# A three-hop graph kernel: a group's relation rows and mask move from SyncE's queue to ScalarE's, and ScalarE's step distances grow by three

## The reference

```python
for _ in range(N_HOPS):                       # 3
    h = agg[head]
    t = agg[tail]
    left = h @ q_w
    right = jnp.tanh(rel * t @ k_w)           # rel = edge_emb[edge_type]
    att = jnp.sum(left * right, axis=1)
    e = jnp.exp(att - segment_max(att, head)[head])
    w = e / segment_sum(e, head)[head]
    summed = segment_sum(w[:, None] * rel * t, head)
    agg = summed / jnp.maximum(cnt, 1.0)[:, None]
    agg = agg / jnp.maximum(jnp.linalg.norm(agg, axis=1, keepdims=True), 1e-12)
    out = out + agg + entity_emb
```

## Time and profile before

| | |
|---|---|
| median of three runs | 11539.55 us |
| span of the profiled execution | 11570.2 us |
| PE busy | 8077.2 us (70%) |
| DVE busy | 6642.3 us (57%) |
| POOL busy | 6401.1 us (55%) |
| ACT busy | 6199.6 us (54%) |
| hop 0, first to last mask operation (L1839, 416 of them) | 3015 to 5782 us |
| hops 1 and 2, first to last copy of relation rows (L1944, 832 of them) | 5874 to 11483 us |

### The profile page before, as it was taken

How to read it: one execution, slowest core, us unless ns; L and a number is a source line. 1 busy time by engine, 2 the same in 40 slices (tenths; PEclk the granted TensorE clock), 3 DMA queues, 4 the chain that set the end, 5 groups by cost and what they waited for, 6 DMA issues and landing times. The chain is left out here.

```text
span 11570.2 us, 241070 instructions
## 1 busy us (share of the span) xinstructions
PE 8077.2 (70%) x47197; PEld 6146.6 (53%) x47197; DVE 6642.3 (57%) x27980; ACT 6199.6 (54%) x15908; POOL 6401.1 (55%) x6757
## 2 busy tenths in 40 slices
PE   2666666666688888888866666666666666666665
PEld 2444444444466666666645555555554555555554
DVE  4666666665555565655655555555554555555556
ACT  1666666666355555555545555555554555555554
POOL 4566666664455555555545555555545555555553
PEclk8776677767788999999978888888888888888887
DMA  2111111111455555555544444444434444444443
GB/s 68 43 43 43 43 43 42 43 43 41 123 176 176 177 176 176 177 175 176 176 124 139 138 138 138 137 139 136 138 118 134 136 138 137 138 136 136 137 136 112
DMA packets 1180950, 1401.16 MB, mean 121 GB/s; under 512 B 216215, under 2 KB 883640, under 8 KB 1180472
## 3 DMA queue, kind: packets, MB, share of 16 engines
q1 hardware_dynamic: 963734, 951.33, 25.8%
q0 software_dynamic: 216064, 444.28, 14.2%
q10 hardware_dynamic: 876, 2.56, 0.1%
HBM read 888.87 MB, written 183.76 MB: 93 GB/s over the span
## 5 line engine op out<-in xcount | busy, mean ns | idle before, releaser
L622 POOL DMA_INDIRECT tails<-node_rows,idx x4992 | 4715.4, 945 | 3803.9 <-remote 1610.6
L1798 DVE SCALAR_TENSOR_TENSOR acc<-acc,fade,banks 128x129 f32 x4992 | 1741.7, 349 | 2100.6 <-remote 1310.5
L1902 PE MATMUL banks<-rt,weight_t 128*128 128x129 f32 x9984 | 1674.8, 315 | 749.1 <-DVE acc L1798 724.3
L622 POOL DMA_INDIRECT l_rows<-in_x_dram,l_idx x1664 | 1591.9, 957 | 1075.1 <-issue 453.6
L1951 ACT ACTIVATE weight<-att,low 128x128 f32<-128x128 f32 x4992 | 1593.0, 391 | 1058.6 <-DVE low L1822 577.1
L1902 PEld LDWEIGHTS banks<-rt,weight_t 128*128 128x128 f32 x9984 | 1483.3, 223 | 849.8 <-issue 795.8
L1887 PE MATMUL banks<-rtt,k_sb 128*128 128x512 f32 x2496 | 1505.3, 685 | 533.8 <-issue 441.7
L1872 PE MATMUL banks<-right,window 128*128 128x128 f32 x9984 | 1567.3, 307 | 281.8 <-DVE tile_low L1814 163.4
L1814 DVE CUSTOM_DVE_ANT_0 att<-banks,agg 128x128 f32<-128x128 f32 x4992 | 1152.8, 287 | 982.6 <-remote 768.9
L1872 PEld LDWEIGHTS banks<-right,window 128*128 128x128 f32 x9984 | 1430.9, 221 | 358.3 <-DVE tile_low L1814 227.5
L1929 ACT ACTIVATE right<-banks 128x512 f32<-128x512 f32 x1248 | 730.5, 585 | 809.3 <-remote 639.2
(11 more groups left out here) (317 smaller groups left out, 9961.5 us busy)
## 6 DMA issues: line engine op xcount, KB each, us to landing
window<-qt SPq DMA_DIRECT2D x4992, 64.0 KB
agg<-pairs_kept SPq DMA_DIRECT2D x832, 384.0 KB
pairs_kept<-agg SPq DMA_DIRECT2D x416, 384.0 KB
rows_in<-tile_rows SPq DMA_DIRECT2D x208, 512.0 KB
tails<-node_rows,idx POOLq DMA_INDIRECT x4992
l_rows<-in_x_dram,l_idx POOLq DMA_INDIRECT x1664
node_rows<-agg SPq DMA_DIRECT2D x6, 1024.0 KB, 6.0
node_rows<-agg SPq DMA_DIRECT2D x3, 1088.0 KB, 8.2
```

The lines of the kernel that those rows point to most:

```text
L622: e.indirect_dma_start(out=rows[:, g, t, :], out_offset=None, in_=of, in_offset=bass.IndirectOffsetOnAxis(ap=idx[:, b, first + t:first + t ...
L1798: e.scalar_tensor_tensor(to, to, fade[:, g2, t:t + 1], bank[b_acc + t // 2][:, t % 2 * WIDE:t % 2 * WIDE + WIDE], ALU.mult, ALU.add).then_ ...
L1902: mm = s.e.matmul(bank[b_acc + t // 2][:, t % 2 * WIDE:t % 2 * WIDE + WIDE], weight_t[:, s.slot(lag, 2), t, :], rt[:, s.slot(lag, RING), t ...
```

## The change

SP's pair load (hops 1 and 2) and pair store (hop 0) become `load_pair` and `store_pair` in `scalar_hop`, issued from ACT. In hops 1 and 2 the load stands last in ACT's step at lag 0, and all other lags of ACT grow by three: so the load of group `i` is issued three of ACT's steps ahead of the copy of group `i`. In hop 0 ACT's lags stay, and the store is at lag 3 in place of 5. The store's semaphores form a ring of eight in place of four, ACT's pipeline is written for one more step of depth, and `scalar_q` gets a closing wait, since ACT may now load into `agg`'s memory only after PE has read it.

```diff
                 def sync_hop(s):
-                    if s.live(0):
+                    if first and s.live(0) and s.i % 2 == 0:
                         g4 = s.slot(0, UNROLL)
-                        if first:
...
-                        else:
-                            g8 = s.slot(0, RING)
-                            of = kept(s, 0)
-                            s.wait_ge((s_min, done(RING, GROUP)), apart=True)
-                            s.e.dma_start(pair[:, g8, :], of).then_inc(s_pair[g8].h, 16)
...
-                    if first and s.live(5):
-                        g4, g8 = s.slot(5, UNROLL), s.slot(5, RING)
-                        to = kept(s, 5)
-                        s.wait_ge((s_copied, done(5)))
-                        s.e.dma_start(to, pair[:, g8, :]).then_inc(s_keep[g4].h, 16)
...
-                        s.wait_ge((s_row[g4 // 2], ring_count(lag, UNROLL, 16)), (s_keep[g4], ring_count(lag + RING, UNROLL, 16)))
+                        s.wait_ge((s_row[g4 // 2], ring_count(lag, UNROLL, 16)), (s_keep[g8], ring_count(lag + RING, RING, 16)))
...
+                def store_pair(s, lag):
+                    if s.live(lag):
+                        g8 = s.slot(lag, RING)
+                        to = kept(s, lag)
+                        s.wait_ge((s_copied, done(lag)))
+                        s.e.dma_start(to, pair[:, g8, :]).then_inc(s_keep[g8].h, 16)
+
+                def load_pair(s, lag):
+                    if s.live(lag):
+                        g8 = s.slot(lag, RING)
+                        of = kept(s, lag)
+                        s.wait_ge((s_min, done(lag + RING, GROUP)), apart=True)
+                        s.e.dma_start(pair[:, g8, :], of).then_inc(s_pair[g8].h, 16)
+
                 def scalar_hop(s):
-                    scalar_idx(s, others, idx, s_rt, 2)
+                    scalar_idx(s, others, idx, s_rt, 2 if first else 5)
                     if first:
+                        store_pair(s, 3)
                         tanh(s, 3)
                         fading(s, 5)
                         copy_products(s, 2)
...
                     else:
-                        copy_relations(s, 0)
-                        tanh(s, 4)
-                        fading(s, 7)
-                        copy_weights(s, 7)
-                        exponents(s, 5)
-                        copy_products(s, 2)
+                        copy_relations(s, 3)
+                        tanh(s, 7)
+                        fading(s, 10)
+                        copy_weights(s, 10)
+                        exponents(s, 8)
+                        copy_products(s, 5)
+                        load_pair(s, 0)
...
+                    e.wait_ge(s_qturned.h, s_qturned.at(node_groups))
...
-                        pipeline(e, f"ha{hop}", scalar_hop, z.slot_groups, deep + 2, (TURN, GROUP * TURN) if first else (TURN, 2 * TURN, GROUP * TURN), TURN)
+                        pipeline(e, f"ha{hop}", scalar_hop, z.slot_groups, deep + 3, (TURN, GROUP * TURN) if first else (TURN, 2 * TURN, GROUP * TURN), TURN)
```

More of the change, by code:

```diff
@@ L1706, in _ @@
                     mm.then_inc(s_across.h, 1)
-        s_row = [sem(f"s_row{i}") for i in range(UNROLL)]
+        s_given.base, s_kept.base = 64, 16
+        s_row = [s_given, s_kept]
         s_win = [sem(f"s_win{i}") for i in range(UNROLL)]
@@ L1718, in gnn_two_layers @@
         pairs_kept = dram("pairs_kept", (z.slot_groups * P * KEEP,))
-        s_keep = [sem(f"s_keep{i}") for i in range(UNROLL)]
+        s_keep = [sem(f"s_keep{i}") for i in range(RING)]
         s_copied = sem("s_copied")
@@ L1734, in gnn_two_layers @@
                 rt = tensor(ctx, f"rt{hop}", [P, RING, GROUP, WIDE])
-                s_pair = s_row + s_keep
+                s_pair = s_keep
                 window = tensor(ctx, f"window{hop}", [P, UNROLL, GROUP, P])
@@ L1763, in sync_hop @@
                 def sync_hop(s):
-                    if s.live(0):
+                    if first and s.live(0) and s.i % 2 == 0:
                         g4 = s.slot(0, UNROLL)
-                        if first:
[L1767 to L1771, removed]
-                        else:
-                            g8 = s.slot(0, RING)
-                            of = kept(s, 0)
-                            s.wait_ge((s_min, done(RING, GROUP)), apart=True)
-                            s.e.dma_start(pair[:, g8, :], of).then_inc(s_pair[g8].h, 16)
+                        at = s.at(lambda i: GROUP * 2 * P * i)
+                        s.wait_ge((s_oht, done(UNROLL - 1)))
+                        s.e.dma_start(rows_in[:, g4:g4 + 2, :, :, :].rearrange("q u t w p -> q (u t w p)"),
+                                      trows[bass.ds(at, 2 * GROUP * 2 * P)].partition_broadcast(P)).then_inc(s_row[g4 // 2].h, 16)
                     if s.live(2):
@@ L2040, in vector_nodes @@
                             for s in s_keep:
-                                e.wait_ge(s.h, 16 * z.slot_groups // UNROLL)
+                                e.wait_ge(s.h, 16 * z.slot_groups // RING)
                         for a, b in zip(thirds, thirds[1:]):
@@ L2064, in _ @@
                         e.wait_ge(s_qt.h, s_qt.at(node_groups))
-                        pipeline(e, f"hs{hop}", sync_hop, z.slot_groups, deep, (TURN,) if first else (TURN, GROUP * TURN), TURN)
+                        pipeline(e, f"hs{hop}", sync_hop, z.slot_groups, deep, (TURN,), TURN)
                         if first:
                             for s in s_keep:
-                                e.wait_ge(s.h, 16 * z.slot_groups // UNROLL)
+                                e.wait_ge(s.h, 16 * z.slot_groups // RING)
                         if hop < HOPS - 1:
@@ L2103, in gnn_two_layers @@
                     s.base += z.slot_tiles
-                for s in s_row[0:2] + s_keep if first else s_pair:
-                    s.base += 16 * z.slot_groups // (UNROLL if first else RING)
+                for s in s_row if first else ():
+                    s.base += 16 * z.slot_groups // UNROLL
+                for s in s_keep:
+                    s.base += 16 * z.slot_groups // RING
                 for s in s_win:
```

## The result

The changed kernel took 11485.92 us (median of four runs, 11462.44 to 11492.87) beside 11538.52 us of the kernel before (four runs): a ratio of 0.9948, 95% interval 0.9934 to 0.9963. That is 53 us, where 645 were forecast.

A forecast was written before the change was run, and what follows sets the result against it. The prediction took SP's issuing of windows and pair loads as the bound. Gains of 541 us (hops 1 and 2) and 104 us (hop 0) made 645 us, giving 10900 us; 8-in-10 range 10350 to 11600 us.

The forecast's parts named there:

- The pace is common to the hops: Hops 0 and 1 take 6.68 and 6.69 us a group, so something that both share sets the pace.
- SP is a full engine and sets the pace: SP issues windows and loads without semaphore pauses at 6.62 us a group in hop 1, the pace of the hop.
- the term of 541 us: Gain in hops 1 and 2: 0.65 us for each of 832 groups, from 6.69 to 6.04 us.
- ACT's wait for the load is a ceiling of 1033.5 us: Hops 1 and 2: removing ACT's wait before its relation copy can shorten the whole by at most 1033.5 us.
- DVE's floor: DVE needs 3.52 us busy plus 2.09 us of waits expected to stay: 5.61 us a group.
- ACT gains nothing in work: The pair's instructions on ACT cost 0 beyond its idle time of 3.18 us a group; bounds 0 and 1.98 us.
- the sign of being wrong: ACT idle before the relation copy or the tanh for more than before would mean its issues are slow.
- the rival in which ACT pays: The pair's instructions run as slowly on ACT as on SP: 11600 us and above, likeliest 11650; chance 0.15.
- Hop 0: Gain of 0.25 us for each of 416 groups, 104 us, with PE near its own limit there.
- It is hidden: DVE's stalls grow by what ACT's wait loses; time within 0.2% of 11540 us; chance 0.06.
- only the issues are saved: SP saves only the pair's DMA issue time, 283 us and 47 us: 11210 us, stretch 11100 to 11500; chance 0.14.

The follow-up runs named there:

- half of the gathers: Two of POOL's four tail gathers a group left out in the hops: changed kernel 8847.50 us (ratio 0.7666), kernel before 8865.79 us (0.7680).
- quick chip: Chip on which the kernel before takes about 8875 us; both kernels rerun unaltered on one: changed 8867.97 us, before 8872.53 us, ratio 0.9997.
- slow chips: Chips on which the kernel before takes about 11540 us, among them that of the result.
- the leash of 6: Changed kernel, POOL's gathers in the hops waiting for `s_rtt` of six groups back in place of four: 13221.58 us, ratio 1.1468, on a slow chip.
- three gathers: Three of POOL's four tail gathers a group in the hops: kernel before 9977.25 us (0.8648, slow chip), changed kernel 8285.58 us (0.9332, quick chip).

## Why the prediction was wrong

- *The pace is common to the hops.* Right, and the best of its observations. What they share is POOL's four gathers. The prediction named POOL only to reject a rival, and priced it at 0.945 us a gather. From start to start it is 1.25 us, 5.0 us a group: with the pause, the whole pace. The Trainium skill says in Perfetto Trace Analysis, section "GPSIMD Engine Instruction", that such an instruction's duration is unreliable and that start-to-start spacing should be taken. This trace agrees for the gathers: 0.945 us against 1.25.
- *SP is a full engine and sets the pace.* This is the step that failed, and with it the term of 541 us. SP was full since many of its instructions were slow in the stalls. It took 6.62 us a group because the group did; with half of the gathers it does the same work in 4.31 us, and on a quick chip it needs 3.77. Relieved of the load, it waits for PE and for what the profile can't name, 454.5 us of 1800, and the pace fell by 0.10 us a group where 0.65 were forecast. In the profiled runs hops 1 and 2 became 97 us shorter, and hop 0, which was to give 104 us, became 8 us longer. An engine without waits whose work stretches with the stalls isn't thereby the bound.
- *ACT's wait for the load is a ceiling of 1033.5 us.* The wait went, as forecast (9.0 us left, against "under 100"). It was no ceiling of any use: with half of the gathers it fell to 24.9 us with the load still on SP, and on a quick chip to 28.4. That it lay inside of stalls that held PE, DVE and SP too is how I read the timelines.
- *DVE's floor.* 2.09 us of DVE's waits were kept constant and 60% of the remaining idle time was given back. Both were settings without a row behind them. The two waits fell to 390 us in 1800, 1.43 us a group, and the pace by 0.10.
- *ACT gains nothing in work.* Its issue takes 344 ns in the median, as said ("near 0.35"), but the sign of being wrong, more idle time before the tanh, came too. Of its sequencer instructions 398 are now slow in 1800 us, 48 before: the rival in which ACT pays saw that a stall holds ACT too, and overpriced it: it had 11650 us. A wait of ACT's issue behind SP's windows, which that case also names, doesn't show: ACT's issue at 7011.34 lasts its usual 0.34 us while a window's issue of SP, from 7011.42 on, lasts its usual 0.52.
- *Hop 0.* Its wait for `rows_in` is gone and the pace stayed, 6.72 against 6.68 us. The prediction then would have had PE as the bound. PE is that at 4.93 to 5.0 us a group on quick chips or without stalls, not at 6.7.
- *The rivals.* "It is hidden" described what happened: waits elsewhere grew by most of what was lost. It stood at 0.06, and as DVE's waits. That is so in hop 0, where DVE's idle time before `acc` grew by 264 us when the mask's fell by 239; in hops 1 and 2 the waits grew by 693 us of 1024 at ACT's own instructions. The time, 11485.9 us, lies in the range and in the stretch that "only the issues are saved" held from 11100 to 11500 us, but by luck: the 0.34 us of the load's issue would have been worth 283 us, and the whole gained 53.

Why there is a gain at all on slow chips, 6.63 to 6.54 and 6.64 to 6.51 us a group in hops 1 and 2, is argued and not shown: SP has fewer instructions to be slow in a stall, so the windows are ready when it ends. On quick chips, where there is no stall, the gain is 0.

## What to carry to other kernels

A queue that never waits can be a victim: before it is called the bound, look at whether its single instructions have their usual length, and what another engine did while they hadn't. Time DMAs that GpSimd issues from start to start, and lay their runs beside the waits that no releaser explains. And ask whether the profile speaks for more than one chip: here the same program differs by 30% between chips, while the runs of one kernel on one chip lie within 0.4%.

## What the runs showed of the hardware

- On slow chips, many sequencer instructions of SP, DVE and ACT take about 0.7 us in long runs of POOL's indirect gathers, and then hardly any starts: DVE stands idle for up to 12.23 us, and the work goes on 2.0 to 2.4 us after the end of the run's last gather in the three shown. With the leash of 6 the slow instructions are few and the standstill comes earlier. On quick chips 1042 gathers in a row do nothing of the kind. Which part of the chip differs, the runs can't tell, nor, since each chip served in one session, whether it is the chip and not something else of the session.
- Plain DMAs from the same engine, with the same packets and bytes through the same queue, cause none of it on a slow chip (8843 us against 11542). They are also shorter (535 ns against 945) and read rows in sequence, so whether it is the reading of an index, POOL's longer work or the scattered rows that matters stays open.
- TensorE's granted clock is lower where the stalls are: 0.85 of full in hop 1 of the kernel before on a slow chip, 0.77 with the leash of 6, 0.95 with three gathers, 0.99 to 1.00 where nothing stalls. PE is busy for 69% of the time there, for 63% with the leash of 6 (7000 to 8800 us), for 75% with three gathers, and for 82% and more where nothing stalls.
